# Layer 2 experts: fp32 gate and up products replaced by three fp32r products of split operands

## What is computed

```python
scores = jax.nn.softmax(flat_x @ gate_w.T, axis=-1).T
topk_weight, topk_idx = jax.lax.top_k(scores, C)        # C = 256, 16 experts
xg = flat_x[topk_idx]
g = jnp.einsum('ecd,eid->eci', xg, Wg)                  # d = 128, i = 512
u = jnp.einsum('ecd,eid->eci', xg, Wu)
h = jax.nn.gelu(g, approximate=False) * u
eo = jnp.einsum('eci,edi->ecd', h, Wd) * topk_weight[..., None]
flat_out = jnp.zeros_like(flat_x).at[topk_idx.reshape(-1)].add(eo.reshape(-1, d))
```

## Time and profile before

| | |
|---|---|
| median of 3 runs | 1697.86 us (1697.16 to 1700.54) |
| the profiled execution | 1706.63 us, span 1704.9 us |
| TensorE matmuls busy | 1490.4 us, 87% of the span |
| VectorE busy | 1260.4 us, 74% |
| ScalarE busy | 1089.9 us, 64% |
| GpSimd busy | 857.1 us, 50% |
| mean granted TensorE clock | 0.952 of full speed |
| expert stage of layer 2 | first gate product at 1203.9 us, last down products at 1319 us |

### The profile page before, as it was taken

The page is one execution under the profiler, slowest core; times in us unless marked ns, Lnnn a source line. Parts: engine busy times, 40 slices in busy tenths (PEclk is TensorE's granted clock), DMA queues, the critical chain, the costliest instruction groups (busy, mean ns, idle before and its releaser), DMA issues. The chain is left out here.

```text
span 1704.9 us, 29946 instructions
## 1 busy us (share of the span) xinstructions
PE 1490.4 (87%) x11248; PEld 1197.3 (70%) x11248; DVE 1260.4 (74%) x2770; ACT 1089.9 (64%) x2122; POOL 857.1 (50%) x798
## 2 busy tenths in 40 slices
PE   6999999999999999899848888845999379998997
PEld 4788887888788887687737676834788256666675
DVE  6999999999999999435461677589433887777772
ACT  4888888888888888455445565632444456666665
POOL 4556576667666666720363744624666632233211
PEclk9999999999999999999779999957999699999999
DMA  3656666656666565300044000040465200000000
GB/s 94 124 103 115 106 120 100 120 108 114 115 108 103 99 105 106 87 1 1 18 137 129 26 2 2 2 133 1 112 148 109 64 1 1 2 2 2 2 2 26
DMA packets 334417, 117.09 MB, mean 69 GB/s; under 512 B 281008, under 2 KB 326096, under 8 KB 334144
## 3 DMA queue, kind: packets, MB, share of 16 engines
q1 hardware_dynamic: 323664, 101.54, 29.2%
q0 software_dynamic: 8496, 12.59, 3.4%
q10 hardware_dynamic: 2112, 1.05, 0.2%
HBM read 37.53 MB, written 10.49 MB: 28 GB/s over the span
## 5 line engine op out<-in xcount | busy, mean ns | idle before, releaser
L2135 ACT ACTIVATE ET_a<-PS 128x256 f32<-128x256 f32 (+2 forms) x512 | 220.5, 499 | 114.8 <-PE PS L2028 72.9
L771 POOL TENSOR_TENSOR dl<-XN,dh 128x1024 f16<-128x1024 f32 x86 | 184.9, 2150 | 155.2 <-DVE D L743 79.7
L205 PE MATMUL PS<-xh,yh 128*128 128x512 f32 x512 | 215.5, 421 | 6.6 <-ACT XNT L608 3.8
L206 PE MATMUL PS<-xl,yh 128*128 128x512 f32 x512 | 204.0, 398 | 0.0
L207 PE MATMUL PS<-xh,yl 128*128 128x512 f32 x512 | 202.8, 396 | 0.0
L608 ACT ACTIVATE G<-PS,nm 128x1024 f32<-128x1024 f32 x128 | 143.0, 1117 | 53.4 <-DVE nm L693 37.9
L608 ACT ACTIVATE XNT<-PS,nm 128x1024 f32<-128x1024 f32 x128 | 143.1, 1118 | 52.3 <-DVE nm L693 41.0
L687 DVE TENSOR_REDUCE nm<-PS 128x1 f32<-128x1024 f32 x128 | 156.6, 1223 | 15.7 <-PE PS L207 13.8
L689 DVE TENSOR_REDUCE nm<-PS 128x1 f32<-128x1024 f32 x128 | 156.0, 1219 | 4.7 <-PE PS L207 1.0
L205 PE MATMUL PS<-dth,xnh 128*128 128x256 f16 x512 | 141.0, 275 | 12.0 <-DVE zl L697 12.0
L2323 DVE CUSTOM_DVE_ANT_0 PS<-PS,mk 128x256 f32<-128x256 f32 (+3 forms) x256 | 128.2, 516 | 30.6 <-PE PS L2007 30.2
(11 more groups left out here) (461 smaller groups left out, 4091.1 us busy)
## 6 DMA issues: line engine op xcount, KB each, us to landing
e_wg<-in_WgT SPq DMA_DIRECT2D x16, 256.0 KB
e_wu<-in_WuT SPq DMA_DIRECT2D x16, 256.0 KB
e_wd<-in_WdT SPq DMA_DIRECT2D x16, 256.0 KB
dth<-dh SPq DMA_TRANSPOSE x128, 3.2
dtl<-dl SPq DMA_TRANSPOSE x128, 3.2
m_x_rows<-m_xs SPq DMA_DIRECT2D x1, 1472.0 KB, 4.9
m_xs<-m_x_rows SPq DMA_DIRECT2D x5, 256.0 KB, 4.8
m_y_rows<-m_xs SPq DMA_DIRECT2D x5, 256.0 KB, 2.3
```

Source lines behind the costliest of these rows:

```text
L205: e.matmul(o, l[0], r[0], start=start, stop=False)
L206: e.matmul(o, l[0], r[1], start=False, stop=False)
L771: e.tensor_tensor(self.dl[:, g % 4, :], self.D[g % 3], self.dh[:, g % 4, :], SUB).then_inc(*self.d_low.up(g))
L2135: e.activation(dst, src, ACT.Exp, scale=self.SC, bias=0.0).then_inc(*self.ex.up(it))
```

## The change

The gate and up products of the experts are made by `mm3`. Its operands are made one expert ahead. For expert x+1, ScalarE copies the transposed tokens and the gate weights into fp32r tiles after its GELU of block 1 of expert x, and the up weights after that of block 2 (`high`). VectorE subtracts: after its multiplication of block 2 of expert x it makes the remainders of tokens, gate and up weights (`low`). TensorE waits for these before expert x+1, and for the remainder of the tokens before it transposes the next ones. The split tiles are double buffered, and lie in memory over the buffers of the shared expert, which adds waits for its last down product. The down products stay as they are.

```diff
-        self.XT = [sb(f"XT{i}", [128, 256])[:, :] for i in range(2)]
...
+        with ExitStack() as shared:
+            own = lambda name, shape, dt=F32: k.sb(shared, "e_" + name, shape, dt)
+            self.sr, self.sd = own("sr", [128, 2, 256]), own("sd", [128, 2, 128])
+            self.sh, self.sl = own("sh", [128, 2, 256], F32R), own("sl", [128, 2, 256], F32R)
+            self.shb = [own(f"shb{i}", [128, 2, 512]) for i in range(4)]
+        self.XT = [[sb(f"XT{n}{i}", [128, 256], F32R)[:, :] for n in "hl"] for i in range(2)]
+        self.wgs, self.wus = [[sb(f"{n}{p}", [128, 2, 512], F32R) for p in "hl"] for n in ("wg", "wu")]
...
             if x:
-                q.wait_ge(self.xt, x - 1)
+                q.wait_ge(self.xt_low, x - 1)
...
-            q.wait_ge(self.xt, x)
+            q.wait_ge(self.xt_low, x)
+            q.wait_ge(self.w_low, (x, "u"))
             q.wait_ge(self.in_e[i], (x, 2))
...
-                e.matmul(o[:, 0:256], self.wg[:, i, ms], self.XT[x % 2], start=True, stop=True)
-                e.matmul(o[:, 256:512], self.wu[:, i, ms], self.XT[x % 2], start=True, stop=True).then_inc(*self.up.up((x, m)))
+                mm3(e, o[:, 0:256], [w[:, x % 2, ms] for w in self.wgs], self.XT[x % 2], True, True)
+                mm3(e, o[:, 256:512], [w[:, x % 2, ms] for w in self.wus], self.XT[x % 2], True, True).then_inc(*self.up.up((x, m)))
...
-            e.activation(self.XT[x % 2], k.bank(7)[:, 0:256], ACT.Copy).then_inc(*self.xt.up(x))
+            q.wait_ge(self.sh_down, 3)
+            e.activation(self.XT[x % 2][0], k.bank(7)[:, 0:256], ACT.Copy).then_inc(*self.xt.up(x))
+
+        def high(x, n):
+            i = x % 3
+            q.wait_ge(self.in_e[i], (x, 2))
+            q.wait_ge(self.sh_down, 3)
+            if x >= 2:
+                q.wait_ge(self.up, (x - 2, 3))
+            raw, to = (self.wg, self.wgs) if n == "g" else (self.wu, self.wus)
+            e.activation(to[0][:, x % 2, :], raw[:, i, :], ACT.Copy).then_inc(*self.w_high.up((x, n)))
...
         turn(0)
+        high(0, "g")
+        high(0, "u")
...
                 elif m == 1 and x + 1 < self.E:
                     turn(x + 1)
+                    high(x + 1, "g")
+                elif m == 2 and x + 1 < self.E:
+                    high(x + 1, "u")
...
+        def low(x):
+            i = x % 3
+            q.wait_ge(self.xt, x)
+            q.wait_ge(self.sh_down, 3)
+            e.tensor_tensor(self.XT[x % 2][1], k.bank(7)[:, 0:256], f(self.XT[x % 2][0]), SUB).then_inc(*self.xt_low.up(x))
+            for n, raw, to in (("g", self.wg, self.wgs), ("u", self.wu, self.wus)):
+                q.wait_ge(self.w_high, (x, n))
+                e.tensor_tensor(to[1][:, x % 2, :], raw[:, i, :], f(to[0][:, x % 2, :]), SUB).then_inc(*self.w_low.up((x, n)))
+        low(0)
...
+                if m == 2 and x + 1 < self.E:
+                    low(x + 1)
                 norm(x, m)
```

More of the change, by code:

```diff
@@ L2411, in __init__ @@
         self.yd = [nc.dram_tensor(f"y_rows{i}", [T, 128], F32, kind="Internal").ap() for i in range(2)]
-        self.sr, self.sd = sb("sr", [128, 2, 256]), sb("sd", [128, 2, 128])
-        self.sh, self.sl = sb("sh", [128, 2, 256], F32R), sb("sl", [128, 2, 256], F32R)
-        self.shb = [sb(f"shb{i}", [128, 2, 512]) for i in range(4)]
         self.z = sb("z", [128, NT, 128])
@@ L2500, in __init__ @@
         self.pick = sig("e_pick", range(4))
-        self.xt_pe, self.xt = sig("e_x_turned", range(E)), sig("e_xT", range(E))
+        self.xt_pe, self.xt, self.xt_low = sig("e_x_turned", range(E)), sig("e_xT", range(E)), sig("e_xT_low", range(E))
+        self.w_high, self.w_low = sig("e_w_high", grid(range(E), "gu")), sig("e_w_low", grid(range(E), "gu"))
         self.up = sig("e_up", grid(range(E), range(4)))
```

## The result

The changed kernel takes 1717.64 us (median of 5 runs, 1714.16 to 1718.33), the kernel before 1697.16 us beside it (5 runs, 1695.11 to 1700.54). The ratio is 1.0122 (95% interval 1.0109 to 1.0135), the difference 20.5 us. Forecast were 1713.9 us and a difference of 16.0.

The account below looks back on a forecast made before the run. The prediction took TensorE to bound the expert stage before, and a loop through three engines after. Terms per expert and the start summed to 15.7 us (16.0 unrounded), added to 1697.86 for 1713.9 us; range 1705 to 1726.

Parts of the forecast that it names:

- The loop through three engines: Per expert, TensorE, ScalarE and VectorE wait in turn; TensorE runs dry until the next expert's last remainder.
- N: Expert without side work: loop from TensorE's restart to its next forecast at 6.99 us against 5.46, +1.5.
- A, B and C: Experts with side work: a ScalarE copy, two Relus, or a TensorE product; loops 7.5, 8.1 and 8.55 us.
- the theory: Splits stand behind the running expert's work, so a loop through TensorE, ScalarE and VectorE sets each expert's time.
- With 8.7 for expert 1 that is 18.5: +1.9: Experts 1 and 2 with one-hot and pick work: 18.5 us together against 16.58 before, +1.9.
- the start: First splits before expert 0 (+1.8) and expert 0's loop with a restart (+1.25): together +3.05 us.
- the costs' bounds: Low and high prices for ScalarE copies, VectorE remainders and fp32r matmuls; they give 1705 to 1718 us.
- the clock rival: TensorE's pauses bring half clock in half of each loop's TensorE stretch: +24 us on top, 1738; chance 0.08.
- experts 7 to 12: Types A, B and C twice over: 1.1 + 0.5 + 0.9, twice, +5.0 us.
- One bound: Upper price of one ScalarE 128x512 copy: 0.63 us, as the second Relu's 0.57 plus SBUF.
- Weights late: Rival: weights land 8.2 us after the last issue instead of 4.6; +1 us per expert, 1729; chance 0.03.
- Hidden after all: Rival: last remainder ends before TensorE's own 4.8 us of work; 8.6 us faster, 1689.3; chance 0.05.

Follow-up runs that it names:

- e1: Changed kernel with the token and gate weight remainders moved behind the multiplication of block 1; ratio 1.0060 to the kernel before.
- e2: Changed kernel without weight remainders from expert 2 on, those of experts 0 and 1 used again; ratio 1.0031 to the kernel before.
- e9: Changed kernel with one more unread 128x512 VectorE subtraction per expert ahead of the up remainder; ratio 1.0224 to the kernel before.
- e7: Changed kernel with weight splits behind block 0, token remainder behind block 1, earlier gate and up loads, expert 0's weights first; ratio 0.9955 to the kernel before.
- e6: Changed kernel with 3, 4 and 5 unread products ahead of TensorE's waits in experts 0, 1 and 2; ratio 1.0095 to the kernel before.
- e5: Changed kernel with expert 0's weight splits made before those of its tokens; ratio 1.0099 to the kernel before.
- e8: The early-splits kernel e7 with an expert's three loads again waiting for the down products; ratio 0.9973 to the kernel before.

## Why the prediction was right, and where it fell short

*The sign and the mechanism* hold. The loop through three engines was forecast from rows of before, with 6.99 us for N, and measured as 7.03 and 7.02; of its pieces ScalarE's high part has 0.52, the remainders 0.34, 0.61 and 0.68. A, B and C were put at 7.5, 8.1 and 8.55 and came to 7.51, 8.18 and 8.61. e1, e2 and e9 move, drop or add splits inside the loop, e7 takes them out of it, and the undisturbed loops change as the theory says.

*What failed* is a step of the sum: "With 8.7 for expert 1 that is 18.5: +1.9". It is the price at full clock (e6 has 18.64). In the changed kernel the clock fell in both experts, and the two took 22.99 us. I had given the fall of the clock a case of its own, 0.08, for half of all stretches and +24 us; it came in three experts, of which expert 0 was in the sum, and cost 4.35. That is nearly all of the 4.5 us between the difference of 16.0 and the 20.5 measured. The case had the price of one fall right, 1.6 us (8.63 against 7.02 in e5), and the number of falls wrong. It should have been a term of the likeliest case: the start was forecast at half clock, and the pauses that follow before the restarts of experts 1 and 2 are among the longer ones (1.79 and 2.71 us). The measured time lies in the range, and even 0.4 us inside the 1718 that the costs' bounds gave. That last part is luck: those bounds held nothing for the clock.

The Trainium skill (TensorE: Matmul & The Clock Gate, HAM oscillation) describes a kernel whose TensorE waits for a transfer in every turn of its loop and falls back to half clock in each; its waits are longer than any pause of the changed kernel. The runs here differ: the clock fell behind shorter pauses in experts 1 and 2 of the changed kernel and in four of e9, and it did not fall in experts 3 to 14 of the changed kernel, which idle 1.35 to 1.93 us at nine of twelve restarts and have 1.00 throughout. With one fall of 1.6 us in every expert the time would have been near the clock rival's 1738.

*The start* was forecast at +3.05 and is +3.4. The first product comes 2.1 us later after the copy than before (0.44 to 2.55), not 1.8: the two weight remainders took 0.82 and 0.78 us there, and the sum had 0.60 and 0.68. Of the smaller terms only that of experts 7 to 12 is off by more than 0.15 us: A, B and C were each short by 0.05 to 0.1, 0.4 in all. One bound does not follow from its working: 0.57 and 0.02 for SBUF are 0.59, not 0.63. It decided nothing, since the copy in the loop came to the 0.52 assumed.

*Weights late* was put at 4.6 us of landing against 7.2 of room: no wait for a transfer shows in the changed kernel's loops, and e8, with less room, has one of about 1 us. *Hidden after all* did not hold for this order, but it does in e7: the prediction's point from which it decides, that the loop's part after pair 1 be shorter than what TensorE has there, is what e7 brings about.

*What stays open*: why the clock held in experts 3 to 14 of the changed kernel with idle times as long as that before expert 1, but fell in its expert 2 behind a pause of only 0.81 us, and in expert 14 of e5 behind one of 1.93 us, like those that left it alone. The time between e5's and the changed kernel's ratio (1.0099 and 1.0122) is thus not a clean price of the start.

## What to carry to other kernels

Work that prepares the next step's operands costs what stands behind its last input, not what it takes: put what depends on nothing of the running step (here the weights' splits) ahead, and leave behind the last arrival only the piece that needs it. Three engines with room on average say nothing; add up one turn from restart to restart, and compare it with the bound engine's own work in it. And where a new wait leaves TensorE idle, price the products behind it at both clocks, expert by expert, from what the clock does in like places of the trace.

## What was unexpected of the hardware

The granted clock does not follow from one pause alone. In the changed kernel it fell after 2.71 and 1.79 us and once after 0.81; after 1.93 it stayed there and fell in e5, and in e9 it fell after 1.95 and stayed after 2.52. A few unread products in the pause (e6) kept it at 1.00 in experts 1 and 2. The restart of TensorE has a small price of its own: the timeline has the second matmul 0.20 us behind the first, where later ones start 0.12 apart. The 0.36 of the first in the chain is its whole length, of which 0.28 is the length of every such matmul; the others overlap, so they count 0.12 there.
